# Building the adjacency by windows of five destinations and three tiles, with each tile's one-hot of low source bits made once into a ring of 64 slots

## What is computed

```
src = concat(edge_index[0], loops); dst = concat(edge_index[1], loops)
deg = segment_sum(ones, dst);  norm = rsqrt(deg)[src] * rsqrt(deg)[dst]
h = leaky(batchnorm(x @ W1 + b1)); h = h / |h|
for _ in range(5):
    agg = segment_sum((h @ W)[src] * norm, dst) + bias
    h = leaky(batchnorm(agg))
x = layernorm(x + h / |h|)
x = layernorm(x + edge_attention(x, src, dst, edge_attr))
```

## Time and profile before

| | us |
|---|---|
| median of three runs | 5371.18 |
| lowest, highest | 5368.89, 5371.68 |
| the profiled execution, its span | 5371.2 |
| `prepare`, to the first one-hots | 0 to 308.4 |
| adjacency, to the last product of a window | 308.4 to 1472.2 |
| adjacency, to the start of the next stage | 1515.2 |

### The profile page before, as it was taken

One profiled execution on the slowest core, in us unless ns is written; L12 is line 12 of the kernel. 1 busy time (PEld: TensorE's weight loads), 2 busy tenths in 40 slices (PEclk: granted clock), 3 DMA queues, 4 the chain that ended last, 5 costly groups with the idle time before them and its releaser, 6 DMA issues. The chain is left out here.

```text
span 5371.2 us, 95369 instructions
## 1 busy us (share of the span) xinstructions
PE 3946.3 (73%) x25259; PEld 2539.3 (47%) x25260; DVE 3302.9 (61%) x9981; ACT 1686.0 (31%) x4268; POOL 3612.1 (67%) x4256
## 2 busy tenths in 40 slices
PE   4446666666649999999999677776777776667775
PEld 2212222222224544545454356666666666666664
DVE  5999999999930211202020377777777777777777
ACT  0046666666620000101010143333333333333332
POOL 1057777788777777777710057777777777777773
PEclk9989999999979999999999788899998899989888
DMA  6613232323379999998978344444444444444442
GB/s 257 241 43 126 91 135 91 137 88 111 119 202 334 310 323 320 312 329 299 339 257 291 120 124 128 128 129 128 129 128 128 129 129 129 128 128 128 129 129 80
DMA packets 319595, 940.56 MB, mean 175 GB/s; under 512 B 76889, under 2 KB 144333, under 8 KB 317608
## 3 DMA queue, kind: packets, MB, share of 16 engines
q1 hardware_dynamic: 173648, 615.36, 33.9%
q0 software_dynamic: 145824, 323.92, 21.3%
HBM read 735.23 MB, written 203.77 MB: 175 GB/s over the span
## 5 line engine op out<-in xcount | busy, mean ns | idle before, releaser
L741 POOL DMA_INDIRECT records<-recs,poss x1562 | 1621.8, 1038 | 492.8 <-issue 492.8
L1375 POOL DMA_INDIRECT kv<-kv_table,rec x1664 | 1608.0, 966 | 443.7 <-issue 429.1
L901 PE MATMUL ps<-adj,mh 128*128 128x500 f16 (+1 forms) x6370 | 1315.4, 366 | 0.0
L1413 PE MATMUL ps<-msg,ohf 128*128 128x136 f32 x3328 | 554.0, 315 | 620.3 <-DVE msg L1473 618.6
L573 PE MATMUL ps<-h 128*128 128x490 f16 x2500 | 653.4, 386 | 399.0 <-ACT h L674 367.8
L901 PEld LDWEIGHTS ps<-adj,mh 128*128 128x128 f16 x6370 | 619.8, 97 | 686.3 <-issue 35.6
L1413 PEld LDWEIGHTS ps<-msg,ohf 128*128 128x128 f32 x3328 | 462.6, 209 | 696.1 <-DVE msg L1473 349.5
L528 DVE TENSOR_SCALAR h<-iota,rel 128x490 f16<-128x490 f16 x2500 | 771.1, 369 | 0.0
L1055 DVE SCALAR_TENSOR_TENSOR h<-ps,vecs,deg (+1 forms) x65 | 46.7, 718 | 1122.5 <-PE ps L901 1122.5
L1464 DVE TENSOR_TENSOR kq<-kv,ps 128x512 f32<-128x512 f32 x416 | 285.6, 687 | 561.7 <-DMA kv<-kv_table,rec 544.8
L573 PEld LDWEIGHTS ps<-h 128*128 128x128 f16 x2500 | 201.5, 100 | 850.9 <-ACT h L674 557.0
(11 more groups left out here) (265 smaller groups left out, 4475.8 us busy)
## 6 DMA issues: line engine op xcount, KB each, us to landing
adj<-adj_full SPq DMA_DIRECT2D x420, 875.0 KB, 5.8
adj_full<-blk SPq DMA_DIRECT2D x12, 6125.0 KB, 18.8
records<-deg SPq DMA_DIRECT2D x1, 59840.0 KB, 174.1
rec<-records SPq DMA_DIRECT2D x416, 136.0 KB
recs<-in_edge_attr POOLq DMA_DIRECT2D x142, 352.0 KB, 5.9
kv<-kv_table,rec POOLq DMA_INDIRECT x1664
records<-recs,poss POOLq DMA_INDIRECT x1563
adj<-adj_tail SPq DMA_DIRECT2D x35, 437.5 KB, 3.8
```

The costliest lines, as they stand in the source:

```text
L741: G.indirect_dma_start(out=k.rec_d, out_offset=bass.IndirectOffsetOnAxis(ap=k.poss[:, q, j:j + 1], axis=0), in_=k.recs[:, q, j, :], in_off ...
L901: last = mm(bank, mh[:, part, hi, :], adj[:, c, x * width:(x + 1) * width], start=False, stop=True, skip_group_check=True)
L1375: G.indirect_dma_start(out=kv[:, q, j, :], out_offset=None, in_=k.kv_d, in_offset=bass.IndirectOffsetOnAxis(ap=rec[:, q, j, RD:RD + 1].bit ...
L1413: last = mm(PS[:, 6 + q % S, 0:MW], ohf[:, q, j, :], msg[:, q, j, :], start=(j == 0), stop=(j == GT - 1))
```

## The change

Windows become half as wide: `WD` = 5, `FAST` = 3, 1250 windows in 125 groups of `WPP` = 10. A code has 49 * 5 = 245 columns.

- **Codes**: one comparison (`tensor_tensor`) makes the code one-hots of all three tiles of a window: it compares a constant array laid out as (245 codes, 3 tiles) with the 16-bit codes of three tiles, read again for every code. TensorE then reads a tile's one-hot with a step of three elements. The five small instructions of L519 go; eight constant arrays, made by GpSimd when the stage starts, take the place of the subtraction.
- **Low one-hots**: `spread` makes each tile's one-hot once, at slot `tile & 63` of a ring; 18 are made ahead, and 12 or 13 ahead of each group. TensorE computes the slot's address for each product from the group's table entry. ScalarE's part of this work goes.
- **ScalarE** moves two windows at once (one PSUM bank holds two), and takes the degrees to a small buffer, which SyncE stores block by block.
- **prepare**: the table is made with two scans, ten counting comparisons on VectorE and ten `Sign` activations with an accumulator on ScalarE, in place of 20 passes on VectorE. The 16-bit codes are new.
- **convolve** no longer stores the degrees before it reads them.

```diff
-WD = 10
+WD = 5
-WCODE = 512
-BW = 50
+WCODE = 256
+PH = 8
+BW = 100
-WPP = 5
-FAST = 4
-TW = 16
+WPP = 10
+FAST = 3
+TW = 32
+RING = 64
+AHEAD_LO = 18
+TWO = 25
...
+                for f in range(PH):
+                    nc.gpsimd.iota(codes[:, f, :, :], [[1, WC], [0, FAST]], base=f * WC, channel_multiplier=0,
+                                   allow_small_or_imprecise_dtypes=True)
...
-                def lo_onehots(to, t, n):
-                    V.tensor_tensor(to, iota[:, 0:P].rearrange("p (o c) -> p o c", o=1).broadcast_to([P, n, P]),
-                                    k.loh[:, bass.ds(t, n)].rearrange("p (j o) -> p j o", o=1).broadcast_to([P, n, P]), ALU.is_equal)
...
+                def spread(t):
+                    V.tensor_scalar(ohl[:, bass.ds(t & (RING - 1), 1), :].rearrange("p a c -> p (a c)"), iota[:, 0:P],
+                                    k.lo[:, bass.ds(t, 1)], None, ALU.is_equal)
...
-                        for x in range(WPP):
-                            last = V.tensor_scalar(rel[:, par, x, :], k.code[:, bass.ds(first[x], FAST)], wbase[:, bass.ds(w + x, 1)], None, ALU.subtract)
...
-                            lo_onehots(ohl[:, q, 0:JV[x], :], first[x], JV[x])
...
-                            for j in range(FAST):
-                                last = V.tensor_scalar(ohc[:, q, j, :], iota[:, :], rel[:, par, x, j:j + 1], None, ALU.is_equal)
-                            last.then_inc(ready, 1)
+                            V.tensor_tensor(ohc[:, (w0 + x) % SL, :, :], codes[:, (w0 + x) % PH, :, :],
+                                            k.code16[:, bass.ds(first[x], FAST)].rearrange("p (o j) -> p o j", o=1).broadcast_to([P, WC, FAST]),
+                                            ALU.is_equal).then_inc(ready, 1)
...
                 with v.Fori(0, WP // 4) as i:
                     for h in range(4):
-                        group(v.snap(i * 4 + h), h * WPP % SL, h % 2)
+                        for t in range(tiles[h], tiles[h + 1]):
+                            spread(v.snap(i * (2 * TWO) + t))
+                        group(v.snap(i * 4 + h), h * WPP)
...
+                    first = firsts_of(PE, gr)
...
-                            pe.wait_ge(psum_free, w + 1)
+                            if q % 2 == 0:
+                                pe.wait_ge(put, gr * (WPP // 2) + x // 2 + 1)
                             pe.wait_ge(ready, w + 1)
-                            pe.wait_ge(ready_lo, w + 3)
                             for j in range(FAST):
-                                last = nc.tensor.matmul(PS[:, q, 0:WC], ohl[:, q, j, :], ohc[:, q, j, :],
-                                                        start=(j == 0), stop=(j == FAST - 1))
+                                last = nc.tensor.matmul(banks[:, q * 256:q * 256 + WC],
+                                                        ohl[:, bass.ds((first[x] + j) & (RING - 1), 1), :].rearrange("p a c -> p (a c)"),
+                                                        ohc[:, (w0 + x) % SL, :, j], start=(j == 0), stop=(j == FAST - 1))
```

More of the change, by code:

```diff
@@ L161, in prepare @@
         hf, df, wf = (k.deg[:, TPL * REC + x * TC:TPL * REC + (x + 1) * TC] for x in range(3))
-        tmn, tmx, up, down = (k.h[:, x * TC:(x + 1) * TC] for x in range(4))
+        tmn, tmx, most, least = (k.h[:, x * TC:(x + 1) * TC] for x in range(4))
         hih = sb("hih", [P, TC], FP16)
-        thr = sb("thr", [P, WPP], FP32)
+        thr, over = sb("thr", [P, WPP], FP32), sb("over", [P, WPP], FP32)
         w4 = sb("w4", [P, 8, WPP], FP32)
+        home = sb("home", [P, 1], FP32)
         tab = sb("tab", [P, TW], I32)
@@ L459, in adjacency @@
     SL = 4
[L460 removed]
     GB = BW // WPP
[L462 removed]
+    PUT = 4
     with ExitStack() as s:
@@ L684, in _, with block_of @@
-                block_of(0, 0, BW, None)
-                block_of(1, 1, BW, None)
+                    act.wait_ge(deg_moved[q], 16 * b // 2 + 16 - 8 * q if type(b) is int else 8 * b + 16 - 8 * q)
+                    A.activation(degs[:, q, 0:width], PS[:, 4, 0:width], ACT.Copy, bias=1.0, scale=4.0).then_inc(deg_free, 1)
+                def block_of(q, b, pairs, i):
+                    for y in range(pairs):
+                        if y == 0:
+                            if i is not None:
+                                act.wait_ge(stored[q], 16 * i)
+                            act.wait_ge(summed, b + 1)
+                        put_pair(b * (BW // 2) + y, q, y, (q * (BW // 2) + y) % 4)
+                        if y == 4 and (type(b) is not int or b > 1):
+                            take(b - 2, q, BD)
@@ L693, in _ @@
[L693 to L694 removed]
+                take(NBLK - 1, 1, BD)
+                take(NBLK, 0, BT)
             @block.sync
             def _(sp):
[L698 to L702 removed]
@@ L704, in _ @@
+                for b in range(2):
+                    store(b, b)
+                with sp.Fori(1, NBLK // 2) as i:
+                    for q in range(2):
+                        b = sp.snap(i * 2 + q)
+                        degree(sp.snap(b - 2), q, BD)
+                        store(b, q)
+                degree(NBLK - 2, 0, BD)
+                sp.wait_ge(put, PUT + NW // 2)
                 sp.dma_start(k.a_d[1][0, :, :].rearrange("p (h d) -> p h d", h=NB),
                              blk[:, 0, :].rearrange("p (h d) -> p h d", h=NB)[:, :, 0:BT]).then_inc(stored[0], 16)
+                degree(NBLK - 1, 1, BD)
```

237 lines of the change are left out of this document (118 added, 119 removed).

## The result

The changed kernel takes 6079.73 us (median of 4 runs, 6077.02 to 6081.94), the one before, on the same chip, 5370.09 (5368.89 to 5371.68): a ratio of 1.132, 95% interval [1.131, 1.134]. It is slower by 709.6 us, where I had forecast 355. The direction was right, the time lies outside the range. All of it arises in the adjacency stage.

The account below looks back on a forecast made before the run. GpSimd's scatter (1202 us) and VectorE (1164) bound the adjacency stage closely; after the change, 125 groups at 12.4 us, 1550, start the next stage 357 us later: 5371 + 355 = 5726 us, range 5590 to 5850.

Parts of the forecast that it names:

- The mechanism: Adjacency stage: VectorE's turn between groups and TensorE's windows, paced by register instructions, together set a group's period.
- TensorE's wait: At a group's end TensorE, its four windows and own start done, waits about 0.8 us for VectorE.
- TensorE's register instruction: Each costs TensorE's sequencer 0.10 us, a product next to nothing: 0.95 us a window.
- The comparison: VectorE's comparison of 735 columns: 0.54 us at two columns a cycle, taken, or 0.92 at the slower rate.
- The load of ten: The register load of ten table entries at a group's start: 0.9 us taken, bounds 0.6 to 3.4.
- VectorE's turn: From VectorE's wait for a group's last window until the next group's first can be multiplied: tiles, loads, comparison, 6.6 us.
- The period: Time per group: 6.6 us plus six windows at 0.95, with 0.1 for signals 12.4 us, times 125 groups.
- branches over unrolled code: Part of the rival "more than I count", 20% in all: branches over code three times as long, given no time.
- The constant arrays: GpSimd makes eight arrays of 735 columns before anyone starts: 0.75 us each, 7 us more.
- The tail: From the adjacency stage's last product at 1855 us to the next stage at 1872: 8.6, 3 for degrees, and barrier.
- GpSimd ends the stage before: In the kernel before, GpSimd's scatter ends the adjacency stage at 1510.0 us, VectorE close; a faster VectorE can win 35.
- A third fewer columns compared: Argument for the 6% rival that sequencer work hides and GpSimd ends the stage, at 5326 us.

Follow-up runs that it names:

- a_fixed: The changed kernel with a window's three products reading a fixed zero buffer, so TensorE works out no slot: 6748.6 us, 1.062 of the kernel before.
- a_between: The changed kernel with the next group's tiles made between the comparisons of this group's windows: 5865.7 us, 1.093 of the kernel before.
- a_noelse: The changed kernel without the branch for long windows on VectorE and TensorE: 7110.0 us on a slow chip, 1.120 of the kernel before.
- a_cn: The changed kernel without the long-window branch and with VectorE making the constant arrays: 7418.7 us on a slow chip, 1.093 of the kernel before.
- a_codes: The changed kernel with its eight constant arrays made by VectorE instead of GpSimd: 6006.9 us, 1.119 of the kernel before.
- b_ctl: Control: the kernel before with bounds assertions on the loads on which waits rest: 6387.9 us on a slow chip, 1.0055 of the kernel before.
- a_ctl: Control: the changed kernel with bounds assertions on the loads on which waits rest: 7195.3 us on a slow chip, 1.134 of the kernel before.
- c_static2: The changed kernel with constant ring slots, tiles batched, window slots from the table, VectorE-made constants, 15 scatter rounds: 6781.6 us, 0.996 of the kernel before.

## Why the forecast was wrong

- **The mechanism** was right, shown from both sides: take TensorE's instructions away and the round falls 9.3 us (a_fixed), move VectorE's tiles and it falls 6.4 (59.4 to 53.0, a_between), part of that by the fetch. Neither alone sets the period. TensorE's wait, 0.8 us a group in the forecast, was 1.0 and 1.5 at two ordinary group ends and 3.1 on average (389.3 / 125).
- **TensorE's register instruction**, 0.10 us: right. The row below is 6250 of them; each starts 0.097 behind the last, an address and its product 0.124. A window took 1.03 and not 0.95, since the product's own issue isn't free as I read the earlier trace rows: +0.5 us in six windows.
- **The comparison**, 0.54 or 0.92: 0.67, between the two (0.58 from start to start), so neither the value that the Trainium skill's "VectorE: DVE Perf Modes" (What auto-detection actually checks) gives nor the rate of L508. **The spread**, 0.3: 0.305. **The load of ten**, 0.9: 1.08. The Trainium skill's figure in "Runtime: NRT & Kernel Launch" (Instruction fetch mechanics), 200 ns a register, would have made it 2.0; for a load from entry 0 the trace disagrees. (The skill speaks there of registers loaded from HBM, and this table lies in SBUF.)
- **VectorE's turn**, 6.6: 7.0 (the last wait passed at 1019.1, the next window ready at 1026.1).
- **The period**, 12.4: the step that failed. A quiet group took 13.7, on average 14.9; over 31 rounds (59.9 - 49.6) x 31 = 320 of the 354 us missed. Of these the fetch of VectorE's loop is 140, by a_noelse against a_cn, a term that the sum had at nothing. I had named "branches over unrolled code" among the rivals without a price, because the kernel before showed none: its loop just fitted. Of the other 180, a quiet group's 13.7 against 12.4 makes about 160. From one group's last comparison to the next group's (1019.22 to 1032.75) it goes by the turn, 7.0 for 6.6, six windows, 6.2 for 5.7, and the two handovers, about 0.4 for the 0.1 of "signals". The rest, some 20, is what is left for loads of 3.5 us and more that now and then occur.
- **The constant arrays**, 0.75 each: 3.7. The first product came at 340.9 where the forecast has about 318, 23 us. The nearest row, an iota of 625 fp32 elements at 0.65, was no bound for one in fp16 with an innermost step of zero. a_codes confirms it.
- **The tail**, 17 us to the next stage: 27. I had counted the degrees and the barrier, and left out the store of the last block, which lands 24.9 us after its issue and which the scatter had hidden.
- **Later stages**, 2 less: 711 us at the next stage's start against 709.6 in all. Right.
- **GpSimd ends the stage before**: it does in that profile, 7 us behind the last block's store. So "a faster VectorE can win 35 us" was a wrong reading: with GpSimd done at 1510.0, nothing is won before the scatter itself gets shorter. By the two ends I estimate some 10 us for a shorter scatter alone; no run shows it.
- **The range**: my own bound for the load of ten, 3.4 us, would have put the sum 2.5 x 125, some 310 us, higher, far over the upper end of 5850. The load came out near my value, so this isn't what failed, but the range was tighter than its terms.
- **"A third fewer columns compared"**: for ten destinations VectorE compared 384 + 4 x 490 = 2344 columns and now 2 x 735 + 2.5 x 128 = 1790, a quarter fewer.

```profile
L616 PEldq ALU_OP  x6250: 32/36/36, 340.7 to 2198.9; - x196
```

## What to carry to other kernels

Count register instructions per product on each sequencer before counting columns. Here they cost 0.1 us each and stand in no busy column; with the turn and the fetch they made 13% more time out of a quarter fewer columns, and slots that are constants or come ready from a table gave it back. Work that one engine does behind its last wait belongs between its waits, if a semaphore or a ring lets it. And look at an unrolled loop's branch back before and after: a stall there can come from a few instructions that never run, or go with a few placed ahead.

## What the runs showed of the hardware that I had not expected

- The same loop body of 330 instructions took 2.8 us at its branch back or 0.3, for eight instructions ahead of it (a_noelse, a_cn). Sixteen that aren't executed raised it from 0.30 to 3.5 us (b_ctl).
- A load of registers cost 0.11 us an entry from entry 0 of a table's row and 0.24 from entries 10 and 22.
- On the slower chips single register instructions took 0.7 us, and only while GpSimd's scatter ran (a_ctl, TensorE's address instructions: at most 709 ns against 51 behind it). In the changed kernel, on a faster chip, the same instructions took at most 51 ns with the scatter running. A kernel with 2.7 register instructions a product loses more on such a chip: a_ctl's rounds take 71 us up to 1600 us and 60 behind.
- The same product stream took the same time at either clock level where register instructions set its pace (a window 0.99 and 1.00 us), and 0.61 against 0.50 where they didn't (c_static2).
- GpSimd took 3.7 us for an fp16 iota of 735 elements, VectorE 0.91 for the same array as an addition.
